# Three-tap partial sums right behind each corner-weight multiplication

## The reference, cut to what matters

```
return corner(y0, x0, (1 - wy1) * (1 - wx1)) + corner(y0, x0 + 1, (1 - wy1) * wx1) + corner(y0 + 1, x0, wy1 * (1 - wx1)) + corner(y0 + 1, x0 + 1, wy1 * wx1)
...
return jnp.einsum('nghwpc,nhwgp->nhwgc', samp, mask_sm).reshape(N, H, W, C)
```

## Time and profile before

| | |
|---|---|
| median of three runs | 14606.53 us |
| span of the profiled execution | 9429.1 us (the page gives no other time of it) |
| gathers on POOL | 7056, 6834.3 us busy |
| DVE busy | 6031.0 us |
| ACT busy | 6717.5 us |
| PE busy | 6306.7 us |
| last gather to the end | 373 us |

### The profile page before, as it was taken

How to read it: one execution, slowest core, us unless ns; L and a number is a source line. 1 busy time by engine, 2 the same in 40 slices (tenths; PEclk the granted TensorE clock), 3 DMA queues, 4 the chain that set the end, 5 groups by cost and what they waited for, 6 DMA issues and landing times.

```text
span 9429.1 us, 151169 instructions
## 1 busy us (share of the span) xinstructions
PE 6306.7 (67%) x44945; PEld 3370.3 (36%) x44945; DVE 6031.0 (64%) x17780; ACT 6717.5 (71%) x8200; POOL 6834.3 (72%) x7060
## 2 busy tenths in 40 slices
PE   5556666667766767666666676666676666657786
PEld 3233333333333333333333333333333333333444
DVE  6666666665676666766666666666567666776642
ACT  1368965688756887578866798567875688757891
POOL 5777777777777777777777777777777777777730
PEclk7678887888878888788888888878888888878896
DMA  2222222222222222222222222222222222334535
GB/s 86 70 76 57 58 60 63 84 58 58 62 71 76 58 59 62 74 73 57 59 63 78 67 57 62 62 83 60 57 62 69 78 57 69 97 95 134 151 111 187
DMA packets 453930, 711.90 MB, mean 75 GB/s; under 512 B 146576, under 2 KB 261136, under 8 KB 451472
## 3 DMA queue, kind: packets, MB, share of 16 engines
q0 software_dynamic: 225792, 462.87, 18.4%
q1 hardware_dynamic: 227312, 239.17, 8.0%
HBM read 595.51 MB, written 105.96 MB: 74 GB/s over the span
## 4 chain that ended last, share of the span: by engine, by line
POOL 66%; issue 22%; ACT 4%; DVE 3%; PE 2%; DMA 2%; DVEq 1%; SPq 0%; POOLq 0%; ACTq 0%
POOL pool_mem L1223 66%; ACT tanh L1721 3%; DVE pool_mem L1405 1%; DVEq L1242 1%; PE score_ps L1891 1%; DVE y L1414 1%; PE side_ps L2003 0%; DMA pool_mem<-in_weight 0%; DMA pool_mem<-patches_odd,pool_mem 0%; DMA pool_mem<-patches_even,pool_mem 0%; ACT expo L1731 0%; DMA expert_d<-pool_mem 0%; DVE newton L1276 0%; DVE pool_mem L1337 0%; SPq L1174 0%
## 5 line engine op out<-in xcount | busy, mean ns | idle before, releaser
L1721 ACT ACTIVATE tanh<-key_rep,query 128x896 f32<-128x896 f32 (+7 forms) x6400 | 5530.0, 951 | 1457.6 <-DVEq L1242 978.6
L1223 POOL DMA_INDIRECT pool_mem<-patches_even,pool_mem x3528 | 3414.7, 968 | 1146.5 <-issue 1072.4
L1223 POOL DMA_INDIRECT pool_mem<-patches_odd,pool_mem x3528 | 3419.4, 969 | 1075.7 <-issue 1071.7
L1891 PE MATMUL score_ps<-tanh,score_w 128*32 128x512 f32 (+3 forms) x24320 | 2931.5, 596 | 478.2 <-ACT tanh L1721 474.6
L1405 DVE TENSOR_TENSOR pool_mem<-pool_mem 128x384 f32<-128x384 f32 x2352 | 1141.7, 553 | 1334.3 <-DMA pool_mem<-patches_even,pool_mem 699.2
L1891 PEld LDWEIGHTS score_ps<-tanh,score_w 128*32 128x32 f32 x24320 | 745.9, 120 | 2087.2 <-issue 1386.1
L1414 DVE TENSOR_REDUCE y<-pool_mem 128x64 f32<-128x2304 f32 x392 | 999.6, 2550 | 33.1 <-issue 9.8
L1920 PE MATMUL value_ps<-values,expoT 128*128 128x129 f32 (+1 forms) x5200 | 908.4, 324 | 83.9 <-DVE expoT L1482 71.9
L1920 PEld LDWEIGHTS value_ps<-values,expoT 128*128 128x128 f32 (+1 forms) x5200 | 802.3, 228 | 160.7 <-DVE expoT L1482 100.7
L1276 DVE SCALAR_TENSOR_TENSOR newton<-rstd,newton 128x1 f32<-128x1 f32 (+1 forms) x2403 | 529.2, 220 | 188.1 <-issue 9.8
L1790 PE MATMUL turn_ps<-ident,expo 128*128 128x128 f32 (+1 forms) x2632 | 527.6, 323 | 152.7 <-DVE expoT L1482 128.3
(11 more groups left out here) (168 smaller groups left out, 6035.9 us busy)
## 6 DMA issues: line engine op xcount, KB each, us to landing
pool_mem<-in_weight SPq DMA_DIRECT2D x64, 1024.0 KB, 8.9
pool_mem<-patches_even,pool_mem POOLq DMA_INDIRECT x3528
pool_mem<-patches_odd,pool_mem POOLq DMA_INDIRECT x3528
patches_even<-pool_mem SPq DMA_DIRECT2D x104, 256.0 KB, 2.0
patches_odd<-pool_mem SPq DMA_DIRECT2D x104, 256.0 KB
pool_mem<-in_x SPq DMA_DIRECT2D x56, 224.0 KB
x_tok<-in_x SPq DMA_DIRECT2D x192, 64.0 KB
x_d<-x SPq DMA_DIRECT2D x192, 64.0 KB
```

Of the source, the lines that this page charges most:

```text
L1223: pool.indirect_dma_start(gathered[:, b, j * 4 * CG:(j + 1) * 4 * CG], None, patches_flat[int(odd)], bass.IndirectOffsetOnAxis(ap=index[:, ...
L1721: nc.scalar.activation(tanh[:, TANH_AT[ui][0]:TANH_AT[ui][1]], key_rep[:, lo:lo + w], ACT.Tanh, bias=query[:, col:col + 1]).then_inc(tanh_ ...
L1891: last = mm(score_ps[32 * col:32 * col + 32, ci % 2, lo:hi], score_w[:, place], tanh[:, TANH_AT[ui][0] + lo:TANH_AT[ui][0] + hi], start=pl ...
```

## The change

A small tile `partial` holds six partial sums of 32 channels. In `weigh`, each of the six multiplications is followed by a drain, and each of the first five then by a reduction of its three taps x four corners (384 elements to 32) into `partial`. In `sample`, the sixth piece is reduced, a drain follows, and a last reduction adds the three partial sums of each of the two groups (192 elements to 64) into `y`; it increments `sampled`, and another drain follows. The reduction of 2304 elements is gone. The planner's table is as before, so the order of all queues is too.

```diff
@@ in the declarations
+PIECES = SAMPLES // PIECE
...
+        partial = sb("partial", [P, PIECES, CG])
@@ weigh
-                    for lo in range(0, SAMPLES, PIECE):
-                        part = product[:, lo:lo + PIECE]
-                        v.tensor_tensor(part, part, weight[:, lo:lo + PIECE].unsqueeze(2)
+                    for q in range(PIECES):
+                        taps_ = slice(q * PIECE, (q + 1) * PIECE)
+                        part = product[:, taps_]
+                        v.tensor_tensor(part, part, weight[:, taps_].unsqueeze(2)
                                         .to_broadcast([P, PIECE, CG, 4]), ALU.mult)
-                    settle()
+                        settle()
+                        if q < PIECES - 1:
+                            v.tensor_reduce(partial[:, q], part.rearrange("p t c k -> p c t k"), AX_XY, ALU.add)
@@ sample
                     product = gathered[:, gather_slot(i)].rearrange("p (j c k) -> p j c k", c=CG, k=4)
+                    v.tensor_reduce(partial[:, PIECES - 1], product[:, (PIECES - 1) * PIECE:].rearrange("p t c k -> p c t k"),
+                                    AX_XY, ALU.add)
+                    settle()
                     v.tensor_reduce(y[:, i // 2 % 2, b].rearrange("p (g c) -> p g c", c=CG),
-                                    product.rearrange("p (g t) c k -> p g c t k", g=2), AX_XY, ALU.add)\
+                                    partial.rearrange("p (g q) c -> p g c q", g=2), AX_X, ALU.add)\
                         .then_inc(sampled.sem, 1)
+                    settle()
```

## The result

The change made the kernel slower: 15122.85 us (median of 4 runs, 15096.86 to 15139.79) against 14609.04 us before (4 runs, 14576.27 to 14613.11), a ratio of 1.0348 (95% interval 1.033 to 1.0367). That is 514 us, or 1.31 us for each of the 392 sub-blocks. The forecast was no change.

A forecast was written before the change was run, and what follows sets the result against it. The prediction took POOL's issue of indirect gathers as the bound. Slots 0, gathers -17 and the end +8 us made -9 us, so 14606.5 became 14597 us, called no change (72%), with a range of 14550 to 14690 us.

The forecast's parts named there:

- the first one: Opening step: the 5177 us between traced span and timed runs stay unchanged, so the span's difference is added to 14606.5 us.
- Slots: POOL's gathers waiting for DVE's sums to release gather slots: DVE's lag stays within the spare time, 0 us added.
- the cover: DVE's idle time before the first multiplications, waiting for gathers, that was to hide the added work: 1334 us in all.
- rival (b): DVE bounds the last image, POOL stands at the slots and the end is late: +50 to +78 us, chance 8%.
- Prices: DVE's costs: 0.55 us per 384-element reduction, 0.35 for the last; 1.6 us more per sub-block, 7.1 against 5.5.
- Gathers: Gathers starting within a multiplication are delayed; spacing multiplications at 1.10 us was to change this loss by -17 us.
- the rule: A gather meeting a multiplication waits until 0.425 us after its start; total loss 126 us before, 109 after.
- Rival (c): Gathers get in right after a lone multiplication, so half to all of 132 us goes: about 14510 us, chance 11%.
- rival (d): Every multiplication queues for a gather in flight on the shared port: 3.8 us per sub-block, about 14725 us, chance 1%.
- The end: Work behind the last gather (last weigh, sum, block chain, attention): DVE's lag adds 8 us (0 to 27).
- The net: Sum of the terms for slots, gathers and end, on the span: -9 us, from 9429.1 to 9420 us.
- The bound: POOL's issue of 7056 indirect gathers sets the time, 8978 us from first to last; DVE's weigh and sum are off the path.

The follow-up runs named there:

- g1: The changed kernel, unmodified, against the kernel before in the early regime (before takes about 9420 us): 9429.69 us, ratio 1.0011.
- e6: The changed kernel with 9 of 16 parts of the score sums left out, against the kernel before, early regime: 9435.83 us, ratio 1.0014.
- e1: The kernel before, once more and unchanged, in the late regime: 14839.73 us, ratio 1.0011.
- h2: The kernel before with one multiplication of 2304 elements (18 taps) in place of six, early regime: 9813.76 us, ratio 1.0418.
- e7: The kernel before with each 512-column score matmul split in two of 256, early regime: 9417.86 us, ratio 0.9998.
- e12: The kernel before with 9 of 16 parts of the score sums left out, late regime: 14341.48 us, ratio 0.9694.
- f3: The kernel before with each 512-column score matmul split in two of 256, late regime: 15330.32 us, ratio 1.0358.

## Why the prediction was wrong

*The step that failed* is the first one: "I take what lies around it as unchanged by the edit and add the difference to 14606.5". Next to nothing lies around it: in all 364 executions listed with both numbers 1.8 to 2.6 us lie outside the span (15096.86 and 15095.1; 9429.5 and 9427.7). A span of 9429 us and runs of 14606 us were two different behaviours of one program, and the row that bounded the first (POOL's waits) said nothing of the second. I had written down both numbers and chose the harmless reading.

*Slots.* "These waits follow POOL's clock, so each wipes out lag": true of the early regime, where the 1334 us of idle time in front of the multiplications became 555 in g1 (some 750 forecast) and POOL waited 2 us for a sum, 17 in e6. In the late regime the cover is 24 us, and POOL waits 5851 us for sums: the term "0 (slots)" is what the 514 us replace. POOL standing at the slots is what rival (b) described, but before's own program does so there (e1), from the first image to the last, and DVE isn't full (43% busy): its time lies on a chain of waits between engines.

*Prices.* Right: 0.55 and 0.35 us predicted, 0.553 and 0.374 measured; 1.6 us more for a sub-block predicted, 1.7 measured (7.22 against 5.53). The little that is missing is mainly in the gaps in front of the partial sums (193 us idle, 0.10 us each, not 0.07).

*Gathers.* -17 us predicted for their beat; in the early regime their busy time fell by 16 to 31 us. What gathers lose by starting within a multiplication went from 131 us (before) to 115 (g1), where the rule had 126 and 109. Rival (c), half or all of 132 us gone, didn't come.

The rule of the Trainium skill that rival (d) rests on ("SBUF — State Buffer", section "SBUF: two separate sides": the pair of ports is kept for the whole instruction) agrees with h2 on the gather's side, which waits out 1.35 us of a multiplication but for its last 0.13 us. On the other side it doesn't: this multiplication, started at 4014.63 under a gather in flight from 4014.46 to 4015.40, took 2.56 us, which is the median of the 307 of h2 that started under a gather; the 85 others are no shorter (2.60).

*The end.* 8 us predicted (0 to 27); from e7 to g1 it is 14 + 16 = 30, and 26 to 38 over all pairs of the table: about the whole lag that I had for the last image reaches the end. The rest of 401 us in g1 touches the 400 us that I had named as a sign of (b). The net in the early regime is then +14 by span and +10 by the runs, where I had -9: this term was too small even where the trace fitted, and the forecast of no change held there because the miss stayed under the 44 us.

*The bound.* In the late regime the chain runs through DVE's static order, with TensorE's completions seen late in the middle of it. That DVE's added time costs there, 57 to 78% of it, is shown by four kernels. What makes the completions late isn't settled: it isn't the change (e1), nor this chip or that (one chip had both regimes), nor TensorE's load (e12, f3). Its granted clock is lower in the late regime (0.69 to 0.71 against 0.80 to 0.83); whether that is cause or effect no run shows.

## What to carry to other kernels

Compare the span with the times before anything else. Here they differ by 1.8 to 2.6 us when they belong together; if they differ by thousands, the profile is of another behaviour than the one timed. Look for a bound that would give the time measured, and give it the larger chance. An edit that puts work on an engine "off the path" is free only as long as the path is the one in the trace; where DVE might lie on it, price its added occupancy at half or more (57 to 78% here). Add that occupancy up in order of time: rows that overlap each other count their overlap twice when they are summed.

Where gathers from GpSimd are the bound, keep VectorE's two-operand instructions short (one of 2304 elements cost 395 us there, though it gained 184 in the late regime) and watch the period: a spacing equal to a delayed gather's own period, 1.55 us here, can make one gather after another a delayed one.

## What the hardware showed that I had not expected

- One program, 9420 or 14800 us. In the late regime 26 to 32% of TensorE's semaphore events come over 1 us behind the modelled end of their matmul, against 0.3% at most in the early one; DVE's and ACT's don't. A copy begins 7.7 or 8.4 us behind the matmul it needs, with DVE idle; such waits of the copies reach 37 us. The granted clock of TensorE was 0.823 in g1 and 0.701 in after, but ACT's tanh and DVE's multiplications have the same means in both (951 and 553 ns against 951 and 551).
- A phase lock of two engines: multiplications every 1.55 us make gathers last 1.25 instead of 0.94 us.
- A gather waits for a multiplication until 0.13 us before its end, at both sizes (0.55 and 2.56 us); a multiplication that starts under a gather isn't held.
